# Edge preparation of a four-layer graph kernel: eight chunks staged between the given rows, tile copies two chunks behind, scratch and vectors in two parts

## The chip, the core and the metric

The program runs on one core of a Trainium2 chip. The metric is device time in microseconds (us), the median of repeated runs. The engines are PE (TensorE), PEld (its weight loads), DVE (VectorE), ACT (ScalarE), POOL (GpSimd) and SP (SyncE, which here only issues DMAs). An engine's name with a q at its end is its sequencer issuing a DMA. The lines L... are those of the kernel before.

## The reference, cut to what matters

There are 3125 nodes with 160 features, 100000 edges and four message-passing layers. Only the last steps of each layer differ in formula; all have this form:

```python
h = maximum(layernorm(x), 0)
x = x + layer(h, edge attributes, src, dst)
# in a layer: gather node rows by one index of each edge, weight them by an MLP
# of the edge attributes, multiply with the edge vector, segment_sum by the other index, mix
# layer 0: gathers by dst, sums by src, edge vector = edge_attr_3 / norm(edge_attr_3)
# layers 1 to 3: gather by src, sum by dst; dst comes sorted
```

## The kernel before

The edges stand as a grid of 128 partitions by 782 columns. Sums are made by bins of 32 nodes (100 bins), in tiles of 128 edges of one bin. A group is 8 tiles; there are 110 groups. Layer 0 needs its edge rows (69 words, `rows_a`) in order of `src`, so a preparation sorts them by counting, and scatters them to DRAM. Layers 1 to 3 need the rows (32 words, `rows_b`) in order of `dst`, in which they were given, but padded to whole tiles.

The preparation runs like this.

- DVE and PE: `count(0)` marks, for each of 100 bins, which edges fall in it (DVE, one mark a bin, a ring of 8), and PE sums the marks. Between the marks `vectors` (five steps, after marks 15, 30, 45, 60 and 75) turns the edge vectors `sh` into unit vectors, with a square root of ACT in between, and makes `key_f`. `bases(0)` makes prefix sums. `segment(i)` then ranks a range of columns: `rank` makes, for each of 100 bins, one mark on DVE, one bf16 and one f32 product on PE over the columns of the segment, and one predicated copy on DVE; `positions` turns ranks into slots. Segments are columns of chunks 0 to 3, 4 to 17 and 18 to 33 (`SEGMENTS`), a chunk being 23 columns. After segment 0 come `tiles(0)`, segment 1, `count(1)`, `bases(1)`, `tiles(1)`, segment 2, and the ranking for the other order.
- SP: `stage_rows(c)` loads the 69-word rows of chunk c into one of two buffers, once chunk c - 2 has been scattered. `given(step)` loads a chunk of 32-word rows and stores the chunk before it to `given_dram`. The two are interleaved by hand for chunks 2 to 5: ten given steps and one, then six for each chunk. Then come `bins_out(0)`, `bins_out(1)` and `starts()`, four small transfers with one word a descriptor that SP waits out, and one load back.
- From chunk 6 (`COPY_FROM`) to 33, SP and ACT each issue, for every chunk, 16 DRAM-to-DRAM copies of 128 given rows into tiles (`copy_tiles`); they read the tile starts and the given rows.
- ACT first has 30360 KB of blank rows written to the table that the scatters go to; SP's given rows and POOL's scatters wait for that write (`s_init`). `fill(c)` puts the unit vectors, the index and the key into the staged rows and writes the slots for POOL; `complete(c)` does the like for a given chunk. From chunk 18 it also prepares the node table of layer 0.
- POOL: `scatter(c)` issues 23 indirect DMAs for a chunk, in order, once its fill is done. After chunk 33 it waits for all scatters and copies, reads a flag and signals `s_placed`.
- After `s_placed` DVE clears the accumulator `acc`, all 25600 columns of it, and starts layer 0. Until then `acc` holds the preparation's scratch (`carve`). Each `acc` column is one 32-bit word of each partition.

In each layer POOL gathers rows for the 110 groups (8 indirect DMAs a group, at most two groups ahead), and PE, DVE and ACT work on them in a pipeline. SP loads the rows of group g once the gathers and selections of group g - 2 are done.

```python
acc = sb("acc", [P, BINS * 256])
    dve.wait_ge(s_placed, 1)
    ...
    link(dve.memset(acc[:, :], 0.0))
```

Of the kernel before, what the change touches and what calls it, by code (L numbers as in the profile page):

```python
# [7 lines left out]
I32 = mybir.dt.int32  # L8
# [40 lines left out]
assert BLOCKS % STORES == 0  # L49
R2, R3 = math.sqrt(2.0), math.sqrt(3.0)  # L50
assert COLS % CHUNK == 0 and CHUNKS % 2 == 0 and GROUPS % 2 == 0
SEGMENTS = (0, 4, 18, CHUNKS)
COPY_FROM = 6
GIVEN_FIRST, GIVEN_EACH = 10, 6
assert GIVEN_FIRST + GIVEN_EACH * (COPY_FROM - 2) == CHUNKS
SPREAD = TCOLS * P // (CHUNKS - COPY_FROM)
assert SPREAD * (CHUNKS - COPY_FROM) == TCOLS * P and SPREAD % (2 * GT) == 0
MARKS, PREFIXES, AHEAD = 8, 4, 4
# [1 line left out]
WORK = 2 * PRODS * 320 + 2 * 1024  # L60
assert WORK >= 2 * PRODS * 416 + 2 * 512
PREP_FROM = SEGMENTS[2]
PAD_STEP = NODES // (P * GT)


# [145 lines left out]
def gnn_program(nc, t):  # L211

    ctx = ExitStack()
    with ctx:
# [77 lines left out]
        def carve(words):  # L292
            a = used[0]
            used[0] += words
            assert used[0] <= BINS * 256
            return acc[:, a:a + words]

        even = COLS + COLS % 2
        key_i = [carve(COLS).bitcast(I32) for _ in range(2)]
        key_next = carve(COLS).bitcast(I32)  # L300
        key_f = carve(COLS)
        pos_i = [carve(COLS).bitcast(I32) for _ in range(2)]
        int_a, int_b = carve(COLS).bitcast(I32), carve(COLS).bitcast(I32)
        bin_h = [carve(even // 2).bitcast(BF16)[:, 0:COLS] for _ in range(2)]
        sh = carve(3 * COLS)
# [17 lines left out]
        tile_pad, tile_node = carve(TCOLS), carve(TCOLS)  # L323
        tile_start = carve(TCOLS).bitcast(I32)
        starts_row = carve(TCOLS * P).bitcast(I32)
        falls, unsorted = carve(1), carve(1).bitcast(I32)
        tile_id, tile_bin = carve(TCOLS), carve(TCOLS)
        tile_bin_i = [carve(TCOLS).bitcast(I32) for _ in range(2)]
        stage = [[carve(CHUNK * w) for _ in range(2)] for w in (A_W, B_W)]
        pos_r = [carve(CHUNK).bitcast(I32) for _ in range(2)]  # L330
        blank = [carve(GT * w) for w in (A_W, B_W)]


        s_src = sem("s_src")
# [132 lines left out]
        def copy_tiles(eng, kind, part, c):  # L467

            for v in range(0, SPREAD // 2, GT):
                u = part * (SPREAD // 2) + v  # L470
                _, start = nc.values_load_multi_w_load_instructions(
                    starts_row[0:1, bass.ds((c - COPY_FROM) * SPREAD + u, GT)], engines=(kind,),
                    min_val=0, max_val=P * COLS, skip_runtime_bounds_check_because="clamped to the number of edges")
                for w in range(GT):
                    eng.dma_start(tiles_b[:, bass.ds((c - COPY_FROM) * (SPREAD // GT) + u // GT, 1), w, :],
                                  given_dram[bass.ds(start[w], P), :].unsqueeze(1)).then_inc(s_copy[part], 16)
# [5 lines left out]
        def _(sp):  # L482
# [5 lines left out]
            def stage_rows(c, half, q):  # L488

                wait(sp, s_scat[q], half * (16 * CHUNK))  # L490
                sp.sem_inc(s_apart["sp"], 1)
                sp.dma_start(stage[0][q], t["rows_a"][:, bass.ds(c * (CHUNK * A_W), CHUNK * A_W)]).then_inc(s_stage[0][q], 16)
# [18 lines left out]

            sp.wait_ge(s_init, 16)
            step = 0
            for c in range(2, COPY_FROM):
                for _ in range(GIVEN_FIRST + 1 if c == 2 else GIVEN_EACH):
                    given(step, step // 2, step % 2)
                    step += 1
                stage_rows(c, c // 2, c % 2)
# [81 lines left out]

            def rows_and_tiles(c, half, q):
                stage_rows(c, half, q)
                copy_tiles(sp, SP, 0, c)
            pairs(sp, COPY_FROM, CHUNKS, rows_and_tiles)
            bins_in(0)
            edge_rows(0)
            bins_in(1)
# [166 lines left out]
        def _(act):  # L774
# [2 lines left out]
            act.dma_start(given_dram[P * COLS:, :], blank[1][:, 0:B_W]).then_inc(s_empty, 16)  # L777
            act.dma_start(rows_dram[0].rearrange("(g p t) c -> p g (t c)", p=P, t=GT),
                          blank[0].unsqueeze(1).to_broadcast([P, GROUPS, GT * A_W])).then_inc(s_init, 16)
            act.wait_ge(s_sq, 1)  # L780
            act.activation(norm, norm, ACT.Sqrt).then_inc(s_rt, 1)

            def complete(c, half, q):

# [42 lines left out]
            act.wait_ge(s_dst, 32)  # L827
            act.wait_ge(s_pos[0], 1)
            done = 0
            for c in range(COPY_FROM):  # L830
                if c == SEGMENTS[1]:
                    act.wait_ge(s_pos[0], 2)
                fill(c, c // 2, c % 2)
                if c:
                    for _ in range(GIVEN_FIRST if c == 1 else GIVEN_EACH):
                        complete(done, done // 2, done % 2)
                        done += 1
            assert done == CHUNKS

            act.wait_ge(s_empty, 16)  # L840
            for q in range(2):
# [2 lines left out]

            def fill_and_copy(c, half, q):
                fill(c, half, q)
                copy_tiles(act, ACTIVATION, 1, c)
            pairs(act, COPY_FROM, SEGMENTS[2], fill_and_copy)
            act.wait_ge(s_pos[0], 3)

            act.wait_ge(s_nodes, 32)
# [12 lines left out]
            for c in range(last, last + 2):  # L864
                fill_and_prep(c, c // 2, c % 2)
            pairs(act, last + 2, CHUNKS, fill_and_copy)

            for n in range(4):
                L, S, C = LAYERS[n], s_e[n], s_c[n]
# [115 lines left out]
        def _(dve):  # L985
            links = [0]

            def link(ins):

                links[0] += 1  # L990
                ins.then_inc(s_chain, 1)
                dve.wait_ge(s_chain, links[0])
# [42 lines left out]
                                  ALU.is_equal).then_inc(s_mark, 1)  # L1035
                marked[0] += 1

            def vectors(step):

                if step == 0:  # L1040
                    dve.wait_ge(s_vec, 16)
                    link(dve.tensor_tensor(sh2, sh, sh, ALU.mult))
                elif step == 1:
                    dve.tensor_reduce(norm, sh2.rearrange("p (e c) -> p e c", c=3), AX_X, ALU.add).then_inc(s_sq, 1)
                elif step == 2:
                    dve.wait_ge(s_rt, 1)
                    link(dve.reciprocal(norm, norm))
                elif step == 3:
                    link(dve.tensor_tensor(sh3, sh3, norm.unsqueeze(2).to_broadcast([P, COLS, 3]), ALU.mult))
                elif step == 4:  # L1050
                    link(dve.tensor_scalar(int_b, key_i[0], BIN - 1, None, ALU.bitwise_and))
                    link(dve.tensor_copy(key_f, int_b))

            def count(o):

                link(dve.tensor_scalar(int_a, key_i[o], 5, None, ALU.arith_shift_right))
                link(dve.tensor_copy(bin_h[o], int_a))
                for b in range(BINS):
                    mark(o, b, 0, COLS)
                    if o == 0 and b % 15 == 14:  # L1060
                        vectors(b // 15)

            def bases(o):

# [76 lines left out]
            def segment(i):  # L1141
# [2 lines left out]
                positions(0, a, b)  # L1144
                dve.wait_ge(s_pos[0], i + 1)
            segment(0)
            tiles(0)
            segment(1)

# [15 lines left out]
            statistics()  # L1165
            prep_first()

            for n in range(4):
                L, S, C = LAYERS[n], s_e[n], s_c[n]
                o = 0 if L.rowsA else 1  # L1170
                if n:
                    wait(dve, S["zero"], 1)
                else:

                    dve.wait_ge(s_placed, 1)
                    dve.wait_ge(s_tbd[0], 16)
                    dve.wait_ge(s_tbd[1], 16)
                    dve.wait_ge(s_startd, 32)
                    link(dve.memset(acc[:, :], 0.0))
                if n != 2:  # L1180

                    for q in range(2):
# [531 lines left out]
```

## Time and profile before

| what | value |
|---|---|
| median of 3 runs | 6038.6 us (6031.11 to 6040.99) |
| the profiled execution | 6039.14 us, of it the span 6037.4 us |
| busy share of the span | PE 75%, PEld 65%, DVE 56%, ACT 57%, POOL 70% |
| mean granted TensorE clock | 0.833 of full |
| chain that ended last | POOL 26%, issue 17%, PE 15%, DMA 13%, DVE 5% |

A busy share is an average over the preparation, the four layers and the steps between layers; what a change in one stage is worth is read in that stage. "Issue" is time in which an engine waited for nothing that the profile shows. Each engine works in program order, so a wait of one instruction holds all that stand behind it.

### The profile page before, as it was taken

The page shows a single profiled execution, that of the slowest core. Times are in us where ns is not written, and L with a number is a line of the kernel's source. Part 1 is how long each engine was busy: PE and PEld are TensorE (multiplying, and loading weights), DVE is VectorE, ACT ScalarE, POOL GpSimd, SP SyncE. Part 2 cuts the span into 40 slices and gives each one's busy share as a digit, 9 for nine tenths or more (in the row PEclk, how much of TensorE's full clock was granted, in tenths as well). Part 3 has the DMA queues.
Part 4 walks back from the last instruction along what each step waited for, and adds up shares of the span by engine and source line. Part 5 has one row for each costly group of instructions (what it writes and reads, how often), then busy time and mean ns, then how long its engine had stood idle before and what let it go on. Part 6 is the DMA issues. An engine that isn't in the chain of part 4 may idle for free.

```text
span 6037.4 us, 112434 instructions
## 1 busy us (share of the span) xinstructions
PE 4551.9 (75%) x24536; PEld 3911.6 (65%) x24536; DVE 3374.1 (56%) x10505; ACT 3437.0 (57%) x14704; POOL 4216.1 (70%) x4431
## 2 busy tenths in 40 slices
PE   8893122199999998899999985444444788888887
PEld 6552011199988887788888874444444777777776
DVE  8994000288777776566666673222222456666666
ACT  0000000066666665688888866666666577777774
POOL 4757777677777772677777747777777377777773
PEclk7996555599999999999999995555555799999998
DMA  8622333244444441233333323333333123333331
GB/s 283 192 67 72 75 83 79 56 93 93 93 93 93 93 93 26 75 78 78 78 78 78 78 54 79 78 78 78 78 78 78 40 75 78 78 78 78 78 78 45
DMA packets 660123, 507.08 MB, mean 84 GB/s; under 512 B 445302, under 2 KB 563333, under 8 KB 659894
## 3 DMA queue, kind: packets, MB, share of 16 engines
q0 software_dynamic: 195888, 316.94, 21.0%
q1 hardware_dynamic: 381782, 148.41, 10.5%
q10 hardware_dynamic: 82352, 40.52, 2.3%
q8 instruction: 46, 0.75, 0.1%
q14 instruction: 55, 0.45, 0.0%
HBM read 423.69 MB, written 96.48 MB: 86 GB/s over the span
## 4 chain that ended last, share of the span: by engine, by line
POOL 26%; issue 17%; PE 15%; DMA 13%; DVE 5%; DVEq 2%; ACT 1%; SPq 1%; POOLq 1%; ACTq 0%
POOL gath L766 26%; DMA gath<-table,rows 11%; PE bank L1582 3%; PE bank L1559 3%; DMA rows<-rows_a 2%; PE bank L1632 2%; PE bank L1584 2%; DVE work L1249 2%; PE bank L1578 2%; PE bank L1624 1%; DVE acc L1233 1%; PE bank L1535 1%; DVEq L1256 1%; DVE work L1245 1%; ACT sel L900 0%
## 5 line engine op out<-in xcount | busy, mean ns | idle before, releaser
L766 POOL DMA_INDIRECT gath<-table,rows x3520 | 3358.2, 954 | 1160.2 <-issue 1016.2
L900 ACT ACTIVATE sel<-acc,rows 128x32 f32<-128x32 f32 x10560 | 2294.4, 307 | 696.8 <-DVE acc L1224 695.5
L1233 DVE TENSOR_TENSOR acc<-acc,bank 128x160 f32 (+1 forms) x3520 | 1208.3, 343 | 1042.1 <-PE bank L1578 684.7
L1582 PE MATMUL bank<-work,sel 128*128 128x160 f32 (+1 forms) x5280 | 1335.0, 334 | 92.2 <-DVE acc L1233 91.4
L1559 PE MATMUL bank<-w,work 128*128 128x224 f32 (+2 forms) x5280 | 1160.3, 342 | 115.6 <-DVE work L1249 107.2
L1584 PE MATMUL bank<-work,sel 128*128 128x160 f32 x5280 | 1150.4, 300 | 0.0
L1559 PEld LDWEIGHTS bank<-w,work 128*128 128x128 f32 (+1 forms) x5280 | 886.3, 190 | 263.6 <-DVE work L1249 196.7
L1582 PEld LDWEIGHTS bank<-work,sel 128*128 128x128 f32 x5280 | 879.4, 190 | 191.2 <-DVE acc L1233 165.7
L697 POOL DMA_INDIRECT rows_a<-acc x782 | 760.2, 972 | 341.9 <-issue 237.2
L1578 PE MATMUL bank<-gath,sel 128*128 128x160 f32 x1760 | 549.1, 493 | 554.9 <-DMA gath<-table,rows 501.8
L1245 DVE TENSOR_TENSOR work<-bank,gath 128x256 f32<-128x256 f32 x1320 | 556.1, 421 | 719.9 <-DMA gath<-table,rows 707.6
L1584 PEld LDWEIGHTS bank<-work,sel 128*128 128x128 f32 x5280 | 909.8, 190 | 45.7
L1249 DVE TENSOR_TENSOR work<-bank,gath 128x192 f32<-128x192 f32 (+1 forms) x2640 | 896.4, 381 | 0.0
L1578 PEld LDWEIGHTS bank<-gath,sel 128*128 128x128 f32 x1760 | 462.2, 330 | 641.6 <-issue 614.2
L900 ACT ACTIVATE sel<-sel,rows 128x32 f32<-128x32 f32 x2640 | 581.9, 309 | 50.4 <-DVE sel L1224 48.1
L883 ACT ACTIVATE work<-bank 100x512 f32<-100x512 f32 (+1 forms) x440 | 250.9, 596 | 332.8 <-PE bank L1532 225.3
L818 ACT ACTIVATE acc<-acc 128x69 f32 (+1 forms) x34 | 9.3, 273 | 672.9 <-DMA acc<-in_rows_a 557.0
L1460 PE MATMUL bank<-acc,ident 100*128 100x391 f32 (+3 forms) x1000 | 374.5, 475 | 0.0
L1413 PE MATMUL bank<-ident,sel 128*64 128x128 f32 x25 | 10.2, 406 | 452.5 <-ACT sel L801 452.5
L1413 PEld LDWEIGHTS bank<-ident,sel 128*64 128x64 f32 x25 | 4.3, 174 | 455.7 <-issue 455.6
L878 ACT ACTIVATE attrT<-bank 128x256 f32<-128x256 f32 (+1 forms) x330 | 145.3, 440 | 225.4 <-PE bank L1522 206.3
L1122 DVE COPY_PREDICATED acc<-work,bank 128x391 f32<-128x391 int16 (+3 forms) x500 | 253.1, 506 | 34.0 <-PE bank L1460 29.6
(227 smaller groups left out, 3579.1 us busy)
## 6 DMA issues: line engine op xcount, KB each, us to landing
gath<-table,rows POOLq DMA_INDIRECT x3520
rows<-rows_b SPq DMA_DIRECT2D x330, 128.0 KB
rows_a<-acc ACTq DMA_DIRECT2D x1, 30360.0 KB, 101.7
rows<-rows_a SPq DMA_DIRECT2D x110, 256.0 KB
acc<-in_rows_a SPq DMA_DIRECT2D x34, 793.5 KB, 4.8
acc<-in_rows_b SPq DMA_DIRECT2D x34, 368.0 KB, 3.7
rows_given<-acc SPq DMA_DIRECT2D x34, 368.0 KB
rows_a<-acc POOLq DMA_INDIRECT x782
```

The lines of the kernel that those rows point to most:

```text
L697: pool.indirect_dma_start(rows_dram[0][:, :], bass.IndirectOffsetOnAxis(ap=pos_r[q][:, u:u + 1], axis=0), stage[0][q][:, u * A_W:(u + 1) * ...
L766: pool.indirect_dma_start(gath[q][:, u, :], None, table_dram[n][:, :], bass.IndirectOffsetOnAxis(ap=flat[:, u * w + first:u * w + first + ...
L900: i = act.activation(sel[q][:, t, at:at + BIN], hot, ACT.Copy, scale=e[:, k:k + 1])
L1122: dve.copy_predicated(pos_f[:, lo:hi], mask, bank(4 + r % PREFIXES, P, 0, hi - lo)).then_inc(s_pick, 1)
L1233: dve.tensor_tensor(sums, sums, bank(6 + b, P, 256 * h, 256 * h + L.width), ALU.add).then_inc(S["fl"].sem, 1)
L1245: dve.tensor_tensor(ps, wt[:, :, 0:128].rearrange("p h (w c) -> p h w c", w=2), two[:, :, 0:S0].unsqueeze(2).to_broadcast([P, 2, 2, S0]), ...
L1249: ins = dve.tensor_tensor(pv, wt[:, h, 128:L.wcols].rearrange("p (w m) -> p w m", w=nv) .unsqueeze(2).to_broadcast([P, nv, 3, V1]), two[:, ...
L1460: pe.matmul(out, ident[0:BINS, b:b + 1].to_broadcast([BINS, P]), base[o][0:BINS, lo:hi], start=False, stop=True).then_inc(s_prefix, 1)
L1559: ins = pe.matmul(bank(4 + u % 2, P, 224 * h, 224 * h + L.wcols), hid, w, start=True, stop=True, skip_group_check=True)
L1578: ins = pe.matmul(out, sel[qv][:, t, 0:128], gath[qv][:, t, :], start=True, stop=True, skip_group_check=True)
L1582: pe.matmul(out, sel[qv][:, t, 96:224], work[:, a + NF:a + NF + L.width], start=True, stop=False, skip_group_check=True)
L1584: ins = pe.matmul(bank(6 + b, P, 256 * h, 256 * h + NF), sel[qv][:, t, 0:128], work[:, a:a + NF], start=False, stop=True, skip_group_check ...
```

## The change

SP stages chunks 2 to 7 between the given rows, with four given steps for each chunk after the first eleven, in place of chunks 2 to 5 with six. Segment 0 becomes chunks 0 to 7 (184 columns in place of 92) and segment 1 chunks 8 to 17 (230 in place of 322). The tile copies are still 28 rounds of 32, but the round that went with chunk c now goes with chunk c + 2, and the last two follow chunk 33 on SP and on ACT. `vectors` takes a column range: columns 0 to 183 in `count(0)` as before, columns 184 to 781 in one run after segment 0; ACT takes the second square root after the fill of chunk 1, ahead of its first `complete`. The scratch is carved in another order, so that all that is in use until the last scatter lies in columns 0 to `placing` - 1 (by the widths, 2 x 23 x 69 + 2 x 23 x 32 + 2 x 23 + 8 x 69 + 8 x 32 + 782 + 1 = 6283), and DVE clears the rest once the fills and copies are done, the first 6283 after `s_placed`.

```diff
-SEGMENTS = (0, 4, 18, CHUNKS)
+SEGMENTS = (0, 8, 18, CHUNKS)
 COPY_FROM = 6
-GIVEN_FIRST, GIVEN_EACH = 10, 6
+BEHIND = 2
+GIVEN_FIRST, GIVEN_EACH = 10, 4
+VEC_CUTS = (0, SEGMENTS[1] * CHUNK, COLS)
...
+        stage = [[carve(CHUNK * w) for _ in range(2)] for w in (A_W, B_W)]
+        pos_r = [carve(CHUNK).bitcast(I32) for _ in range(2)]
+        blank = [carve(GT * w) for w in (A_W, B_W)]
+        pos_i = [None, carve(COLS).bitcast(I32)]
+        unsorted = carve(1).bitcast(I32)
+        placing = used[0]
...
-            for c in range(2, COPY_FROM):
+            for c in range(2, SEGMENTS[1]):
                 for _ in range(GIVEN_FIRST + 1 if c == 2 else GIVEN_EACH):
...
                 stage_rows(c, half, q)
+                copy_tiles(sp, SP, 0, c - BEHIND)
+            pairs(sp, SEGMENTS[1], CHUNKS, rows_and_tiles)
+            for c in range(CHUNKS - BEHIND, CHUNKS):
                 copy_tiles(sp, SP, 0, c)
-            pairs(sp, COPY_FROM, CHUNKS, rows_and_tiles)
...
+            def roots(i):
+                a, b = VEC_CUTS[i], VEC_CUTS[i + 1]
+                act.wait_ge(s_sq, i + 1)
+                act.activation(norm[:, a:b], norm[:, a:b], ACT.Sqrt).then_inc(s_rt, 1)
+            roots(0)
...
-            for c in range(COPY_FROM):
-                if c == SEGMENTS[1]:
-                    act.wait_ge(s_pos[0], 2)
+            for c in range(SEGMENTS[1]):
                 fill(c, c // 2, c % 2)
+                if c == 1:
+                    roots(1)
                 if c:
...
             assert done == CHUNKS
+            act.wait_ge(s_pos[0], 2)
...
                 fill(c, half, q)
-                copy_tiles(act, ACTIVATION, 1, c)
-            pairs(act, COPY_FROM, SEGMENTS[2], fill_and_copy)
+                copy_tiles(act, ACTIVATION, 1, c - BEHIND)
+            pairs(act, SEGMENTS[1], SEGMENTS[2], fill_and_copy)
...
             pairs(act, last + 2, CHUNKS, fill_and_copy)
+            for c in range(CHUNKS - BEHIND, CHUNKS):
+                copy_tiles(act, ACTIVATION, 1, c)
...
                     if o == 0 and b % 15 == 14:
-                        vectors(b // 15)
+                        vectors(0, b // 15)
...
             segment(0)
+            for step in range(5):
+                vectors(1, step)
             tiles(0)
             segment(1)
...
+            dve.wait_ge(s_fill[0], 4 * CHUNKS)
+            for q in range(2):
+                dve.wait_ge(s_copy[q], 16 * TCOLS * P // 2)
+                dve.wait_ge(s_tbd[q], 16)
+            dve.wait_ge(s_startd, 32)
+            link(dve.memset(acc[:, placing:], 0.0))
...
                     dve.wait_ge(s_placed, 1)
-                    dve.wait_ge(s_tbd[0], 16)
-                    dve.wait_ge(s_tbd[1], 16)
-                    dve.wait_ge(s_startd, 32)
-                    link(dve.memset(acc[:, :], 0.0))
+                    link(dve.memset(acc[:, 0:placing], 0.0))
```

## Rows read from the trace of the kernel before

**Rows 1.** Timeline of POOL: start, duration, operation, idle before it and its releaser.

```profile
127.53 1.10 POOL L697 DMA_INDIRECT rows_a<-acc  x1 [67.81 <-ACT acc L824]
...
342.38 0.97 POOL L697 DMA_INDIRECT rows_a<-acc  x1 [35.27 <-ACT acc L824]
...
1160.76 0.97 POOL L697 DMA_INDIRECT rows_a<-acc  x1 [0.30 <-issue]
```

**Rows 2.** Groups of POOL by line, 1160 to 2400: layer 0's gathers, busy, then idle.

```profile
L766 POOL DMA_INDIRECT gath<-table,rows x880 | 842.5, 957 | 289.7 <-issue 249.0 <-DMA rows<-rows_a 40.1 <-DVE work L1249 0.6
```

**Rows 3.** Timeline of DVE in count(0): three of the vector passes and the first scan.

```profile
15.67 2.60 DVE L1042 TENSOR_TENSOR acc<-acc 128x2346 f32<-128x2346 f32 x1
...
30.82 5.04 DVE L1047 RECIPROCAL acc<-acc 128x782 f32<-128x782 f32 x1
...
49.19 0.56 DVE L1051 TENSOR_SCALAR acc<-acc 128x782 int32<-128x782 int32 x1
...
60.57 1.22 DVE L1066 TENSOR_TENSOR_SCAN work<-bank,acc 100x512 f32<-100x512 f32 x1 [0.63 <-PE bank L1439]
```

**Rows 4.** Timeline of DVE in segment 0, with 92 columns.

```profile
65.33 0.86 DVE L1034 TENSOR_SCALAR work<-acc,iota_bins 128x92 bf16<-128x92 bf16 x5
...
67.08 0.26 DVE L1122 COPY_PREDICATED acc<-work,bank 128x92 f32<-128x92 int16 x1 [0.17 <-PE bank L1460]
67.25 0.24 DVE L1034 TENSOR_SCALAR work<-acc,iota_bins 128x92 bf16<-128x92 bf16 x1
```

**Rows 5.** Stretches: length, busy and count of PE, PEld, DVE, ACT, POOL; granted clock, DMA.

```profile
100.00:124.00 24.00, 24.00 (x126) 23.92 (x125) 16.26 (x79) 0.00 (x0) 0.00 (x0) 0.50 0.16 55
...
134.00:150.00 16.00, 16.00 (x71) 9.83 (x70) 15.60 (x47) 1.06 (x6) 12.24 (x13) 0.99 0.62 170
...
5000.00:5100.00 100.00, 88.85 (x537) 78.42 (x537) 63.65 (x218) 76.92 (x339) 75.78 (x80) 1.00 0.31 78
```

**Rows 6.** Timeline of PE and DVE in segment 1, with 322 columns.

```profile
130.66 0.47 PE L1459 MATMUL bank<-work,acc 128*128 128x322 bf16 x1
...
132.01 0.47 PE L1459 MATMUL bank<-work,acc 128*128 128x322 bf16 x1
...
161.00 0.52 DVE L1122 COPY_PREDICATED acc<-work,bank 128x322 f32<-128x322 int16 x1
...
161.41 0.29 DVE L1034 TENSOR_SCALAR work<-acc,iota_bins 128x322 bf16<-128x322 bf16 x1
161.62 0.52 DVE L1122 COPY_PREDICATED acc<-work,bank 128x322 f32<-128x322 int16 x1
```

**Rows 7.** Timeline of SP's DMA issues in the preparation.

```profile
104.47 0.81 SPq L499 DMA_DIRECT2D acc<-in_rows_b  x2
...
172.89 0.37 SPq L492 DMA_DIRECT2D acc<-in_rows_a  x1
...
270.02 0.37 SPq L492 DMA_DIRECT2D acc<-in_rows_a  x1
...
299.27 12.92 SPq L534 DMA_DIRECT2D tile_bins<-acc  x2
321.05 0.36 SPq L548 DMA_DIRECT2D tile_starts<-acc  x1
...
336.51 0.41 SPq L492 DMA_DIRECT2D acc<-in_rows_a  x1
...
1104.84 0.34 SPq L492 DMA_DIRECT2D acc<-in_rows_a  x1
1106.13 13.30 SPq L475 DMA_DIRECT2D rows_b<-rows_given  x16
```

**Rows 8.** Timeline of all engines at the start of layer 0.

```profile
1169.26 21.39 DVE L1179 MEMSET acc<- 128x25600 f32 x1 [127.62 <-issue]
...
1187.19 0.96 POOL L766 DMA_INDIRECT gath<-table,rows  x1 [0.30 <-issue]
...
1203.76 0.95 POOL L766 DMA_INDIRECT gath<-table,rows  x1 [15.61 <-DMA rows<-rows_a]
```

More of the change, by code:

```diff
@@ L51 @@
 assert COLS % CHUNK == 0 and CHUNKS % 2 == 0 and GROUPS % 2 == 0
-SEGMENTS = (0, 4, 18, CHUNKS)
+SEGMENTS = (0, 8, 18, CHUNKS)
 COPY_FROM = 6
-GIVEN_FIRST, GIVEN_EACH = 10, 6
-assert GIVEN_FIRST + GIVEN_EACH * (COPY_FROM - 2) == CHUNKS
+BEHIND = 2
+GIVEN_FIRST, GIVEN_EACH = 10, 4
+assert COPY_FROM + BEHIND == SEGMENTS[1] and GIVEN_FIRST + GIVEN_EACH * (SEGMENTS[1] - 2) == CHUNKS
 SPREAD = TCOLS * P // (CHUNKS - COPY_FROM)
@@ L298, in gnn_program @@
         even = COLS + COLS % 2
+        stage = [[carve(CHUNK * w) for _ in range(2)] for w in (A_W, B_W)]
[4 more added lines that the diff above has]
+        placing = used[0]
+        pos_i[0] = carve(COLS).bitcast(I32)
         key_i = [carve(COLS).bitcast(I32) for _ in range(2)]
@@ L301, in gnn_program @@
         key_f = carve(COLS)
-        pos_i = [carve(COLS).bitcast(I32) for _ in range(2)]
         int_a, int_b = carve(COLS).bitcast(I32), carve(COLS).bitcast(I32)
@@ L325, in gnn_program @@
         starts_row = carve(TCOLS * P).bitcast(I32)
-        falls, unsorted = carve(1), carve(1).bitcast(I32)
+        falls = carve(1)
         tile_id, tile_bin = carve(TCOLS), carve(TCOLS)
         tile_bin_i = [carve(TCOLS).bitcast(I32) for _ in range(2)]
-        stage = [[carve(CHUNK * w) for _ in range(2)] for w in (A_W, B_W)]
-        pos_r = [carve(CHUNK).bitcast(I32) for _ in range(2)]
-        blank = [carve(GT * w) for w in (A_W, B_W)]
         s_src = sem("s_src")
@@ L779, in _ @@
                           blank[0].unsqueeze(1).to_broadcast([P, GROUPS, GT * A_W])).then_inc(s_init, 16)
-            act.wait_ge(s_sq, 1)
-            act.activation(norm, norm, ACT.Sqrt).then_inc(s_rt, 1)
+            def roots(i):
[3 more added lines that the diff above has]
+            roots(0)
             def complete(c, half, q):
@@ L1036, in mark, with vectors @@
                 marked[0] += 1
-            def vectors(step):
+            def vectors(i, step):
+                a, b = VEC_CUTS[i], VEC_CUTS[i + 1]
+                some, squares = sh[:, 3 * a:3 * b], sh2[:, 3 * a:3 * b]
                 if step == 0:
                     dve.wait_ge(s_vec, 16)
-                    link(dve.tensor_tensor(sh2, sh, sh, ALU.mult))
+                    link(dve.tensor_tensor(squares, some, some, ALU.mult))
                 elif step == 1:
-                    dve.tensor_reduce(norm, sh2.rearrange("p (e c) -> p e c", c=3), AX_X, ALU.add).then_inc(s_sq, 1)
+                    dve.tensor_reduce(norm[:, a:b], squares.rearrange("p (e c) -> p e c", c=3), AX_X, ALU.add).then_inc(s_sq, 1)
                 elif step == 2:
-                    dve.wait_ge(s_rt, 1)
-                    link(dve.reciprocal(norm, norm))
+                    dve.wait_ge(s_rt, i + 1)
+                    link(dve.reciprocal(norm[:, a:b], norm[:, a:b]))
                 elif step == 3:
-                    link(dve.tensor_tensor(sh3, sh3, norm.unsqueeze(2).to_broadcast([P, COLS, 3]), ALU.mult))
+                    link(dve.tensor_tensor(sh3[:, a:b, :], sh3[:, a:b, :], norm[:, a:b].unsqueeze(2).to_broadcast([P, b - a, 3]),
+                                           ALU.mult))
                 elif step == 4:
-                    link(dve.tensor_scalar(int_b, key_i[0], BIN - 1, None, ALU.bitwise_and))
-                    link(dve.tensor_copy(key_f, int_b))
+                    link(dve.tensor_scalar(int_b[:, a:b], key_i[0][:, a:b], BIN - 1, None, ALU.bitwise_and))
+                    link(dve.tensor_copy(key_f[:, a:b], int_b[:, a:b]))
             def count(o):
```

## The prediction

> **What bounds the kernel now.** I read the preparation and the start of layer 0 only, since nothing behind them is edited. First POOL's timeline: 782 scatters run from 127.53 to 1161.73 with one hole, 35.27 us ahead of chunk 6 [rows 1]. Chunks 6 to 33 take (1161.73 - 342.38) / 28 = 29.26 us each; chunks 0 to 5 take (342.38 - 35.27 - 127.53) / 6 = 29.9 us each, with their small waits. So the preparation ends at: first scatter, plus 34 chunks, plus hole. DVE reaches its clearing of `acc` after idling 127.62 us [rows 8], so neither it nor the ranking for the other order sets the end; POOL does.
>
> The hole is SP's: chunk 6 is loaded at 336.51, after the given rows and the four one-word transfers, 299.27 to 336.51 [rows 7]. POOL starts 342.38 - 336.51 = 5.87 us after that load is issued.
>
> The first scatter waits for `count(0)`, `bases(0)` and segment 0 on DVE and PE, one behind the other; it can't start before the blank rows are written, about 104.47, when SP's loads start [rows 7].
>
> At the other end the clearing, 21.39 us, starts 7.5 us after the last scatter's end, and the gathers of group 2 idle 15.61 us because their rows wait for selections, which wait for the clearing [rows 8]. Later in layer 0 POOL idles little but for issue: 40.1 us on rows in all, of which 15.6 are that one wait [rows 2]. So a start that comes sooner should reach the end of the layer.
>
> **First scatter.** The vector steps in `count(0)` are three passes of 2.60, one of 5.04, two of 0.56, 13.96 us in all [rows 3] (the reduction and the scaling read as many elements as the first pass). On 184 of 782 columns that is 3.3, with some 0.15 fixed for each of six 4.0. Saved: 10.0 us. DVE stays the bound of the count: the marks between take it longer than they take PE, and only the ring's few waits are left. Ranking then starts at 65.33 - 10.0 = 55.3 [rows 4].
>
> A ranking step with 92 columns takes 24.0 / 42 = 0.57 to 0.58 us (126 products, three a step), PE and its weight loads filling the time at granted clock 0.50, the 1.2 GHz level [rows 5]; 100 steps are 58.0 us, and 127.53 - 65.33 - 58.0 = 4.2 us are head, positions, fill and issue. For 184 columns no row exists. At the low level a step of 322 columns takes 132.01 - 130.66 = 1.35 us [rows 6], and by columns 184 take 0.77. At the high level DVE is the longer one: its copy takes 0.17 us at 92 [rows 4] and 0.41 at 322 [rows 6], so 0.27 at 184; its mark takes (0.86 - 0.24) / 4 = 0.155 at 92 and 0.21 at 322, so 0.18; together 0.45. PE would want 0.38. So segment 0 is 77 us at the low level and 45 at the high. Which? The 92-column steps never left the low level; the 322-column steps began at it and were at 0.99 from 134 on [rows 5], a few us after the first of them. In time by columns 184 at the low level is 0.77 us of streaming without room for more, as at 322, and unlike 92, where the loads filled the step. I take the high level after six steps at the low one: 6 x 0.77 + 94 x 0.45 = 46.9, and 4.7 for the rest (positions are twice as wide). First scatter: 55.3 + 46.9 + 4.7 = 106.9, just past the floor of 104.47. Gain 20.6 us; the bounds are +22 and, at the low level throughout, -9.5 (137.0).
>
> The second part of the vectors, 598 columns, some 11 us, runs after segment 0. Behind it on DVE are `tiles(0)` and segment 1, which chunk 8 needs 240 us later: covered. ACT's second root stands ahead of the first `complete`, behind two passes of 2.0 us, so the given rows start some 4 us later against the first scatter. They were ten steps and 172.89 - 127.53 = 45.4 us to chunk 2's load; now 49.1, plus 5.9 to the scatter, is 55.0 where chunk 2 is due at 59.8. Covered, thinly. That DVE's passes slow the scatters beside them costs 0 to 4 us; I take 0, as the pace of 29.9 has DVE's work in it.
>
> **The hole.** Between the loads of chunks 2 and 5 three cycles of six given steps take (270.02 - 172.89) / 3 = 32.4 us [rows 7], so four take 21.6, less than a chunk's scatter: each load now waits for its buffer instead. Chunk 7 is loaded when chunk 5 is scattered, at 106.9 + 6 x 29.9 + 1.6 = 287.9 (1.6 is from the scatter's end to the load, as at 1104.84 = 1161.73 - 2 x 29.26 + 1.6). Four given steps follow, two thirds of 299.27 - 270.02, 19.5: 307.4. Then the one-word transfers: 37.2 us before, but the first of them, with scatters beside it, took 12.5 us where the second took 8.9 (321.05 - 299.27 - 12.92, with its issue 9.2) [rows 7]. Now all have scatters beside them. Bounds: 37 and 50; I take 41.8. Chunk 8 is loaded at 349.2 and scattered from 355.1. It is due at 106.9 + 8 x 29.9 = 346.1. Hole: 9.0 us in place of 35.3. From there 26 x 29.26 = 760.8: end 1115.9, 45.8 us sooner than 1161.73.
>
> Tile copies do not open the hole again: 1.3 + 13.3 us a round [rows 7] in 29.26. The last two rounds stand behind chunk 33's load, 56.9 us before POOL ends: SP is through three rounds after 43.8 us, ACT, whose fill comes first, after some 48.4, and landed by some 51. POOL's wait for copies is covered by about 6 us.
>
> **The clearing.** 21.39 us for 25600 columns is 0.836 ns each: 16.1 us for the first 19317, 5.3 for the last 6283. The first part starts some 6 us before POOL ends (P) and ends at P + 10.1, past `s_placed` at P + 7.5; the second ends at P + 15.6 where the clearing ended at P + 28.9. Gain 13.3 us, of at most 16.1; group 2's gathers keep 2.3 us of their 15.61.
>
> The Trainium skill, "VectorE: DVE Perf Modes", section "Zero memsets can be issued as uint32 (trn2)", says that a memset takes one cycle per element; that would be an estimated 20.1 and 6.5 us at its 0.96 GHz, and a gain of some 8 in place of 13.3. The row of 21.39 us decides against it.
>
> **Sum.** 45.8 + 13.3 = 59.1 us from the profiled execution's 6039.1, which stands within 0.5 us of the median 6038.6: 5980.
>
> **The rivals.**
> - The clock stays low in segment 0: first scatter at 137.0, all else as above: 5980 + 30 = 6010. For it: the 92-column steps, low from end to end. Against: 322. Chance 0.15.
> - The change moves the hole rather than closing it: given steps or one-word transfers stretch beside the scatters (six given steps took 32.4 us in the mean of three cycles and 29.3 in the last, so the pace is not fixed). At 50 us for the transfers 5988; if the whole 35.3 us came back, 6006. Chance 0.12.
> - DVE's first clearing stops POOL's scatters: up to 16 us, 5996. Against: a gather during the clearing took 0.96 us, its usual 957 ns [rows 8, 2]. Chance 0.03. By the Trainium skill, "SBUF — State Buffer", section "Who interferes with whom", a DVE instruction with at most one SBUF input does not contend outside its two-port modes; the trace agrees.
> - Slower than before: a layer that now comes 59 us sooner loses the high clock. Layer 3 has PE at 88.85 us of 100 at clock 1.00 [rows 5]; at the low level the same work is 177.7, so each 100 us cost 78 more, and from 76 us at the low level the gain is gone: 200 us would give 6136. Against: those loops aren't edited. Chance 0.03.
>
> My forecast has 0.67. The range holds the forecast's own bounds (22 in place of 20.6 for the first scatter, a hole of 4, all 16.1 of the clearing: 5971, with a few us of spread), and reaches over the first rivals: 5967 to 6012. A measurement of this kernel tells 0.2%, 12 us, from no change; beyond that on the fast side lie nearly all cases: faster 0.94, same 0.02, slower 0.04.
>
> **What would show it.** POOL's first scatter near 107 (137: the clock); DVE's copies of 184 columns every 0.45 us from about 61; SP's load of chunk 8 near 349 and the idle ahead of POOL's next scatter under 15 us; scatters ending near 1116; two memsets of 16 and 5 us, the second ending 16 us after the last scatter; every layer as long as before. A hole over 20 us, or a first scatter past 115, makes the sum wrong.

## The result and the profile after

| | before | changed | predicted |
|---|---|---|---|
| median | 6036.13 us (4 runs beside it) | 5985.23 us (4 runs, 5982.02 to 5992.07) | 5980 |
| ratio | 1 | 0.9917 [0.99, 0.9934] | 0.990 |
| profiled execution, span | 6039.14, 6037.4 us | 5982.02, 5980.4 us | |
| mean granted TensorE clock | 0.833 | 0.838 | |
| first scatter | 127.53 | 107.07 | 106.9 |
| hole: idle ahead of the first scatter behind the one-word transfers | 35.27 | 7.66 | 9.0 |
| last scatter ends (P) | 1161.73 | 1114.48 | 1115.9 |
| clearing ends behind P | 28.9 | 21.4 | 15.6 |

The kernel is faster by 0.8%: 50.9 us by the medians, where the sum said 59.1. The profiled executions differ by 57.1 us, because the one before stood 3.0 us above its median and the changed one 3.2 below its own. Positions below are those of the profiled executions. The table's lower four rows tell where the sum held and where it did not: three of them are within 1.5 us, the last is off by 5.8.

POOL's timeline in the changed kernel, the rows that answer to [rows 1] and [rows 8]:

```profile
107.07 1.23 POOL L704 DMA_INDIRECT rows_a<-acc  x1 [44.54 <-ACT acc L834]
...
353.65 0.97 POOL L704 DMA_INDIRECT rows_a<-acc  x1 [7.66 <-ACT acc L834]
...
1113.52 0.97 POOL L704 DMA_INDIRECT rows_a<-acc  x1 [0.30 <-issue]
...
1149.23 0.95 POOL L773 DMA_INDIRECT gath<-table,rows  x1 [8.59 <-DMA rows<-rows_a]
```

The first row came 20.5 us sooner, the hole shrank by 27.6, and P came 47.25 us sooner, 0.8 us less than their sum. The idle ahead of group 2's gathers, 15.61 us before, is 8.59 where 2.3 was forecast.

DVE's timeline from the end of the count to the second part of the vectors:

```profile
39.36 8.45 DVE L1047 TENSOR_SCALAR work<-acc,iota_bins 128x782 bf16<-128x782 bf16 x25
48.47 1.23 DVE L1082 TENSOR_TENSOR_SCAN work<-bank,acc 100x512 f32<-100x512 f32 x1 [0.66 <-PE bank L1461]
...
53.12 0.97 DVE L1047 TENSOR_SCALAR work<-acc,iota_bins 128x184 bf16<-128x184 bf16 x5
...
57.87 0.37 DVE L1138 COPY_PREDICATED acc<-work,bank 128x184 f32<-128x184 int16 x1 [0.29 <-PE bank L1482]
58.13 0.26 DVE L1047 TENSOR_SCALAR work<-acc,iota_bins 128x184 bf16<-128x184 bf16 x1
58.58 0.37 DVE L1138 COPY_PREDICATED acc<-work,bank 128x184 f32<-128x184 int16 x1 [0.18 <-PE bank L1482]
...
60.98 0.37 DVE L1138 COPY_PREDICATED acc<-work,bank 128x184 f32<-128x184 int16 x1
61.24 0.26 DVE L1047 TENSOR_SCALAR work<-acc,iota_bins 128x184 bf16<-128x184 bf16 x1
61.45 0.37 DVE L1138 COPY_PREDICATED acc<-work,bank 128x184 f32<-128x184 int16 x1
...
103.37 0.26 DVE L1145 CAST acc<-acc 128x184 int32<-128x184 f32 x1
...
105.30 2.03 DVE L1057 TENSOR_TENSOR acc<-acc 128x1794 f32<-128x1794 f32 x1
...
117.26 0.26 DVE L1103 COPY acc<-bank 128x100 f32<-128x100 f32 x1
```

The first scan starts 12.1 us sooner than in [rows 3] (10.0 in the sum), and the 100 steps of segment 0 take from 53.12 to 103.37, 50.2 us (46.9 in the sum). The second part of the vectors takes 105.30 to 117.26, behind segment 0, as said.

DVE's groups by line in the changed kernel, 50 to 104 (busy, mean ns of one, then idle):

```profile
L1138 DVE COPY_PREDICATED acc<-work,bank 128x184 f32<-128x184 int16 x100 | 36.5, 365 | 2.5 <-PE bank L1482 2.1
L1047 DVE TENSOR_SCALAR work<-acc,iota_bins 128x184 bf16<-128x184 bf16 x100 | 26.3, 266 | 0.0
```

Stretches of the same kernel (PE, PEld, DVE, ACT, POOL, granted clock, DMA):

```profile
55.00:60.00 5.00, 5.00 (x26) 4.13 (x24) 3.65 (x15) 0.00 (x0) 4.34 (x9) 0.67 1.09 372
60.00:65.00 5.00, 5.00 (x37) 4.26 (x36) 5.00 (x22) 0.00 (x0) 2.12 (x6) 1.00 1.06 385
65.00:103.00 38.00, 37.59 (x243) 26.69 (x241) 37.29 (x159) 0.00 (x0) 0.00 (x0) 1.00 1.02 365
```

Here the choice between the two levels of the clock can be read: it rises inside the first stretch, with PE busy throughout, and stays at 1.00, the 2.4 GHz level, to the end of the segment. The rows before show the same from DVE: in the first steps its copy waits for PE, 2.1 us in all; from about 59 on it waits for nothing and starts a copy every 0.47 us.

SP's issues around the old hole, answering to [rows 7]:

```profile
306.21 13.80 SPq L539 DMA_DIRECT2D tile_bins<-acc  x2
330.86 0.36 SPq L553 DMA_DIRECT2D tile_starts<-acc  x1
331.27 0.56 SPq L554 DMA_DIRECT2D tile_first_node<-acc  x1
345.52 0.29 SPq L556 DMA_DIRECT2D acc<-tile_starts  x1
347.99 0.40 SPq L497 DMA_DIRECT2D acc<-in_rows_a  x1
```

From 306.21 to 347.99 are 41.8 us, the value taken (the load back of the starts is in it); chunk 8 is loaded 1.2 us sooner than forecast.

The chain that ended last, at the clearing, in the changed kernel (start, length, what):

```profile
1106.33 2.34 DMA rows_b<-rows_given
...
1108.92 4.10 issue
1113.02 16.17 DVE acc L1191
1129.19 1.36 issue
1130.55 5.30 DVE acc L1201
```

and the same chain in the kernel before:

```profile
1163.87 5.39 issue
1169.26 21.40 DVE acc L1179
```

The last tile copy had landed at 1108.7, 5.8 us ahead of P; the forecast had 6. But each memset has "issue" ahead of it, 4.10 and 1.36 us, together the 5.5 us that the sum lacks. What that is became the main question.

Layer 0 handed the gain on. The first row of the memset that follows it on POOL, before and after:

```profile
2310.70 2.77 POOL L738 MEMSET acc<- 128x3200 f32 x1 [16.68 <-PE bank L1624]
```

```profile
2255.13 2.77 POOL L745 MEMSET acc<- 128x3200 f32 x1 [16.68 <-PE bank L1646]
```

It starts 55.6 us sooner, where 47.25 + 7.5 = 54.75 came in at the layer's start. No layer lost the high clock that it had before.

### The profile page after: what moved, and what is told of

Its sections match the earlier page's. It is cut to its first block, busy times and chain, and to the rows that moved or that the text cites. A ratio compares the mean times of both kernels' runs of the same rounds, so it can differ in the third digit from the quotient of the medians.

```text
span 5980.4 us, 112354 instructions
## 1 busy us (share of the span) xinstructions
PE 4519.9 (76%) x24536; PEld 3884.8 (65%) x24536; DVE 3365.0 (56%) x10512; ACT 3432.8 (57%) x14705; POOL 4219.0 (71%) x4431
## 4 chain that ended last, share of the span: by engine, by line
POOL 37%; issue 21%; DMA 16%; PE 14%; DVE 7%; DVEq 2%; SPq 1%; ACT 1%; ACTq 1%; POOLq 1%
POOL gath L773 26%; DMA gath<-table,rows 12%; POOL rows_a L704 11%; DMA rows<-rows_a 3%; PE bank L1654 2%; PE bank L1604 2%; DVE work L1271 2%; PE bank L1581 2%; PE bank L1600 2%; PE bank L1606 2%; PE bank L1646 1%; DVE acc L1255 1%; DVE work L1267 1%; DVEq L1278 1%; PE bank L1557 1%
## 5 line engine op out<-in xcount | busy, mean ns | idle before, releaser
L1482 PE MATMUL bank<-acc,ident 100*128 100x391 f32 (+3 forms) x1000 | 349.5, 441 | 0.0
```

Of the source, the lines that this page charges most:

```text
L1482: pe.matmul(out, ident[0:BINS, b:b + 1].to_broadcast([BINS, P]), base[o][0:BINS, lo:hi], start=False, stop=True).then_inc(s_prefix, 1)
```

## The experiments

The kernels come in three sets of four; the first two sets ran on one chip, the third on another. Each set's ratios are against the kernel before in the same set (6038.93, 6036.76 and 6036.36 us). POOL's gathers of layer 0 take 967 to 974 ns on the first chip and 955 to 959 on the second, so positions are compared within a chip. Which chip the result above comes from is not on record. Its gathers (957 ns before, 956 after) and its transfers (41.8 us; 37.7 to 38.7 in five kernels on the first chip, 41.2 and 42.3 in two on the second) are like the second's, and it is compared with that one.

**One part undone at a time** (first set). Segment 0 back to chunks 0 to 3, with eight chunks staged all the same:

```diff
-SEGMENTS = (0, 8, 18, CHUNKS)
+SEGMENTS = (0, 4, 18, CHUNKS)
+STAGED = 8
...
+                if c == SEGMENTS[1]:
+                    act.wait_ge(s_pos[0], 2)
                 fill(c, c // 2, c % 2)
```

> The changed kernel, but segment 0 has 92 columns again (segment 1 has 322); SP still stages chunks 2 to 7, the vectors stay in two parts. Theory (clock): ranking 92 columns stays at the low clock and takes 58 us where 184 columns took 50, so the first scatter comes near 115 in place of 107.07, and all behind it, the scatters' end included, some 8 us later; total about 8 us above the changed kernel. Rival (work): half the columns are half the work, ranking takes about 33 us and the first scatter waits only for the blank rows, near 107; total unchanged.

Measured 5998.76 us, 0.9934 [0.992, 0.9947]. POOL's first scatter, and the stretch of the ranking, in this kernel:

```profile
115.48 1.24 POOL L705 DMA_INDIRECT rows_a<-acc  x1 [51.50 <-ACT acc L835]
```

```profile
65.00:103.00 38.00, 38.00 (x199) 37.81 (x198) 26.90 (x132) 0.00 (x0) 0.00 (x0) 0.50 1.02 366
```

Half the columns take longer: the 92-column steps stay at granted clock 0.50, the 1.2 GHz level, with PE and its loads full, and last 0.58 us where the 184-column steps last 0.47. The hole was only 3.87 us here, so P was 1118.97. The repeat of the changed kernel on this chip (below) has 108.34, 4.85 and 1113.97: 7.1 us at the first scatter became 5.0 at P, the rest was given back by the shorter hole and the pace of the scatters.

The vectors in one part:

```diff
-VEC_CUTS = (0, SEGMENTS[1] * CHUNK, COLS)
+VEC_CUTS = (0, COLS)
...
-            for step in range(5):
-                vectors(1, step)
```

> The changed kernel, but the vectors are made in one part, all columns inside count(0). Theory: the count is bound by DVE, so the first scatter comes 10 us later, near 117, the second root no longer stands ahead of the given rows, the hole ahead of chunk 8 stays 7 to 8 us, total 10 us above the changed kernel. Rival: PE or the blank rows bound the count as well and the first scatter moves by under 4 us.

Measured 6001.35 us, 0.9934 [0.992, 0.9948]; first scatter 119.13, hole 5.10 (7 to 8 was expected, but the repeat has 4.85 too), P 1124.24. Against the same repeat the split is worth 10.8 us at the first scatter and 10.3 at P.

The scratch cleared in one part:

```diff
-            link(dve.memset(acc[:, placing:], 0.0))
...
-                    link(dve.memset(acc[:, 0:placing], 0.0))
+                    link(dve.memset(acc[:, :], 0.0))
```

> The changed kernel, but acc is cleared in one piece after the last scatter. Theory: the clearing ends 28.9 us after the last scatter's end as before, in place of 21.4, the gathers of group 2 idle 15.6 us in place of 8.6, total 7.5 us above the changed kernel. Rival: the start of layer 0 is bound by its gathers and the split is worth nothing, total within 2 us.

Measured 5999.67 us, 0.9932 [0.9919, 0.9946]. P was 1114.17; DVE's timeline:

```profile
1121.69 21.39 DVE L1197 MEMSET acc<- 128x25600 f32 x1 [125.95 <-issue]
```

It starts at P + 7.5 and ends at P + 28.9, as before the change. Against the repeat (P + 21.7) the split is worth 7.2 us at this place, against the profiled changed kernel 7.5, and not the 13.3 of the sum.

The first part cleared without waiting for the tile copies, which takes the row of starts that they read (896 words) into the last part, 7179 columns:

```diff
+        starts_row = carve(TCOLS * P).bitcast(I32)
         placing = used[0]
...
-                dve.wait_ge(s_copy[q], 16 * TCOLS * P // 2)
```

> The changed kernel, but the tile starts that the copies read lie in the part cleared last (7179 columns), so the first clearing (18421 columns) waits for the fills and not for the copies. Theory: it starts 52 us before the last scatter ends and is hidden whole, the second (6.0 us) starts 7.5 us after that end and ends 13.5 us after it, total 7.9 us below the changed kernel. Rival (port): a clearing of 15.4 us beside scatters stops POOL for as long, the chunk it falls in takes 45 us in place of 29.3, total 7 us above the changed kernel.

Measured 5987.79 us, 0.9913 [0.99, 0.9927]. The memsets in this kernel:

```profile
1063.68 15.41 DVE L1190 MEMSET acc<- 128x18421 f32 x1 [70.27 <-issue]
1115.59 6.04 DVE L1200 MEMSET acc<- 128x7179 f32 x1 [36.51 <-issue]
```

The large one now lies 48 us ahead of P (1111.83), beside running scatters. These kept their pace, 13 of them from 1063 to 1079 at 966 ns with 0.30 between: DVE's clearing does not stop POOL's scatters. The clearing ends at P + 9.8, where 13.5 was expected: that took the 7.5 us between P and the memset as fixed, and they became 3.8. The time fell less than expected all the same, as the repeat shows.

**Repeat, and one part alone** (second set).

> The changed kernel once more, on the chip of the three below, so that they are compared with it and not across chips. First scatter near 107, last scatter's end near 1114, clearing done 21.4 us after it; about 0.992 of the time of the kernel before. The four runs of the first call gave 0.9934, 0.9934, 0.9932 and 0.9913; if clear_without_copies is 8 us below this kernel, this one stands near 0.9926, and if the first clearing stood in the way of the scatters there, near or below 0.9913.

Measured 5992.14 us, 0.9922 [0.9909, 0.9936]. First scatter 108.34, hole 4.85, P 1113.97; the clearing again ends 21.7 us behind P, with 1.38 us between its parts. On this chip the four kernels above are thus 6.6, 9.2 and 7.5 us slower and 4.4 us faster than the changed kernel by their medians. They belong to another set, whose kernel before was 2.2 us slower, and by the ratios the intervals overlap, so these differences are good to a few us; the positions in the traces carry the readings. The repeat gained 44.6 us on its kernel before and not 50.9.

> The kernel before with nothing but the other order of the scratch and the clearing in two parts. There the copies are through 42 us before the last scatter ends. Theory: the first clearing (16.2 us) is over before it, the second (5.3 us) ends about 13 us after it in place of 28.9, group 2's gathers wait little; total 14 to 16 us below the kernel before (0.9975). Rival (late copies are no cause): here too the clearing ends 21 us after the last scatter, total 7 us below.

This is the kernel before with the scratch carved in the new order and cleared in two parts. Measured 6024.58 us, 0.9978 [0.9969, 0.9987]. The copies are long done here, so the first part (1121.46) is hidden and the clearing ends at P + 8.9 in place of P + 28.9. P itself was 1153.28 and the hole 27.29 us, though nothing ahead of the clearing was edited but the places in the scratch: SP's transfers began at 293.48, 5.8 us sooner than in [rows 7], and took 33.7 us in place of 37.2. This is the other chip, and no trace of the kernel before was taken there, so whether the chip or the scratch's order makes the 8 us stays open. The total fell by 12.2 us, near the 14 to 16 expected.

**The one-word transfers issued together.** Each order's wait for its bins is moved behind the issue of all four:

```diff
                     sp.dma_start(bins_dram[o].rearrange("(c p) -> p c", p=P), tile_bin_i[o]).then_inc(s_tbd[o], 16)
-                sp.wait_ge(s_tbd[o], 16)
...
             starts()
+            for o in range(2):
+                sp.wait_ge(s_tbd[o], 16)
```

> The changed kernel, but SP issues the four one-word transfers one behind the other and waits once, in place of waiting out each pair. Theory (the hole is the sum of three waits): the transfers take 15 to 25 us in place of 42, chunk 8 is loaded by 331 and waits for nothing, POOL's hole of 7.7 us is gone, all behind it 7 us sooner. Rival (descriptors): the four share the same queue and take their 38 us all the same, hole and total unchanged.

Measured 5986.32 us, 0.9915 [0.9902, 0.9929]. SP's timeline:

```profile
307.37 1.14 SPq L539 DMA_DIRECT2D tile_bins<-acc  x2
308.56 0.71 SPq L552 DMA_DIRECT2D tile_starts<-acc  x1
309.31 0.58 SPq L553 DMA_DIRECT2D tile_first_node<-acc  x1
328.38 0.30 SPq L555 DMA_DIRECT2D acc<-tile_starts  x1
332.82 0.40 SPq L497 DMA_DIRECT2D acc<-in_rows_a  x1
```

With three waits between them (one behind each order's bins, one behind the last two) the four transfers and the load back took 37.7 us in the repeat; beside one another they take 25.5, and the hole is gone: no wait over 0.4 us stands ahead of chunk 8, and P is 1108.70, 5.3 us sooner than in the repeat.

> The changed kernel with both: transfers together, and the first clearing free of the copies. Theory: the two add, the scatters end 7 us sooner and group 2's gathers follow group 1's without a wait, total 15 us below the changed kernel. Rival: one hides the other (gathers of layer 0 bound it from its start), total 8 us below.

These are the transfers together and the first part cleared without the copies. Measured 5982.07 us, 0.9909 [0.9894, 0.9924], 10.1 us under the repeat of the changed kernel, between the theory's 15 and the rival's 8. P came 5.4 us sooner and the clearing's end another 11.9 nearer to it. Layer 0, from P to the memset behind it, took 1151.4 us in the repeat and 1146.45 here: of the 11.9 us 4.9 reached its end. Both mechanisms worked at their own place, but the layer does not hand on the whole of the second.

**Staging alone, and what the clearing waits for** (third set, the other chip).

> The changed kernel with the vectors in one part, the scratch cleared in one part and the old bounds of the segments (0, 4, 18, 40): SyncE's staging and the trailing copies are all that is left of the change. If the three parts add up, the first scatter starts near 127 us and the stop between scatters, 27 to 28 us long before, shrinks to under 6; POOL's scatters then end 20 to 25 us sooner than before's, near 1137 to 1142, the clearing starts 7.5 us behind them as before, and the time is 20 to 30 us below before's, ratio .995 to .997. A rival: the stop stays above 15 us although eight chunks are staged, because the first scatters come as late as before; then the ratio is above .997.

Measured 6008.28 us, 0.9956 [0.9943, 0.997], a little better than expected, though the hole is longer than the 6 forecast: first scatter 127.35, hole 7.75, P 1133.63, 28.1 us sooner, and the medians differ by 28.1 too. Of the 54.75 us at the start of layer 0 staging with the trailing copies thus brings 28.1, and what is left, 1133.63 - 1114.48 = 19.2 at P and 7.5 in the clearing, belongs to the other parts. That this adds up is no test, since the 19.2 is a difference. Undone one at a time on the first chip, the segment and the vectors gave 5.0 and 10.3 at P, and 7.1 and 10.8 at the first scatter, of 20.3 here. The trailing of the copies was never undone by itself.

The next kernel asks whether the 4.1 us ahead of the first memset are the price of DVE's 116 us without work:

```diff
                 copy_tiles(sp, SP, 0, c)
+            sp.sem_inc(s_wake, 1)
             bins_in(0)
...
+            dve.wait_ge(s_wake, 1)
+            link(dve.memset(acc[:, placing:placing + 1], 0.0))
             for q in range(2):
                 dve.wait_ge(s_copy[q], 16 * TCOLS * P // 2)
```

> The changed kernel with one signal from SyncE behind its last tile copy, on which VectorE clears one word before it waits for the rest. Theory: the 4.1 us between the last landing and the first memset is the price of a long sleep, whatever the instruction is; the one word's memset pays it, beginning some 4 us after the signal, near 1108.7, and the first part's memset follows at once, within 1 us of the last copy's landing, 3 to 4 us sooner than in the changed kernel; the clearing ends near 17.5 to 18.5 us behind the last scatter in place of 21.4, and the time falls by 2 to 4 us. Rival: the 4 us is between the copies' landing and what a wait sees of it; then the one word is cleared within 0.5 us of the signal and the first part's memset stays 4 us behind the landing.

Measured 5984.71 us, 0.9918 [0.9904, 0.9931], no change. SP's and DVE's timelines:

```profile
1105.25 0.40 SPq L548 DMA_DIRECT2D tile_bins_row<-tile_bins  x1
```

```profile
1105.32 0.06 DVE L1190 MEMSET acc<- 128x1 f32 x1 [108.12 <-issue]
1112.78 16.16 DVE L1195 MEMSET acc<- 128x19317 f32 x1 [7.40 <-issue]
1130.32 5.29 DVE L1205 MEMSET acc<- 128x6283 f32 x1 [1.38 <-issue]
```

The theory falls. SP signals between its last copy's issue (over at 1105.14) and the issue at 1105.25, and after 108 us without work the one-word memset starts 0.07 us behind the latter. The large one still starts 4.3 us behind the last landing (1108.44); DVE's waits take the first 0.2 of them, and the other 4.10 are "issue", as before. The rival named beside it fits this kernel, but not the one after the next.

> The kernel with both mends, and the same signal from SyncE, some 4 us before the last scatter: VectorE clears one word on it and then waits for POOL. Theory of the long sleep: the one word's memset starts some 4 us behind the signal, the second part's memset within 0.5 us of POOL's mark in place of 3.75 behind it, the clearing ends 6.5 us behind the last scatter in place of 9.8, and the time falls by another 1 to 3 us, since the gathers' pace already sets the layer's start. Rival, the delay belongs to the wait for POOL's mark: the second memset stays 3.7 us behind.

Measured 5973.27 us, 0.9893 [0.9877, 0.9908], no gain over the kernel without it. SP's signal came just ahead of 1098.81 here, 10 us ahead of P and not 4, and the one word was cleared at 1098.88; the second part still started 3.8 us behind P.

> The kernel with both mends once more, for a comparison on the same chip: as before, a ratio of .991 and a second memset that starts 3.75 us behind the last scatter's end.

Measured 5971.29 us, 0.9891 [0.9876, 0.9906], the best of all, 13.4 us under the changed kernel with the one-word memset, measured beside it. The second memset starts 3.77 us behind P, as expected. ACT's last fill and DVE's memsets in this kernel:

```profile
1057.17 0.20 ACT L835 ACTIVATE acc<-acc 128x23 int32<-128x23 int32 x1
```

```profile
1061.28 15.41 DVE L1191 MEMSET acc<- 128x18421 f32 x1 [70.09 <-issue]
1112.98 6.04 DVE L1201 MEMSET acc<- 128x7179 f32 x1 [36.29 <-issue]
1119.24 0.70 DVE L1205 MEMSET sel<- 128x768 f32 x1 [0.23 <-DVE acc L1201]
```

Here the signal is ACT's and no DMA's, and the large memset still starts 1061.28 - 1057.37 = 3.91 us behind the end of ACT's last fill. So the wait for a landing is not it either. What orders all rows is the size of the memset itself:

```
columns   ahead of the row (us)   row (us)   together   what came just before
25600     5.39                    21.39      26.78      POOL's signal
19317     4.10                    16.16      20.26      last copy landed
18421     3.91                    15.41      19.32      ACT's last fill
 6283     1.36                     5.29       6.65      the first part's memset
  768     0.23                     0.70       0.93      a memset
    1     0.07                     0.06       0.13      SP's signal
```

The share ahead of the row is 0.21 to 0.22 ns a column in the four large ones, whoever released them and after 116 us of idle or none. It goes with the memset's size, and the row shows only four fifths of what the memset costs: 26.78 / 25600 = 1.046 ns a column here. The memset of 7179 columns, not in the table, fits: POOL's signal came 2.14 us behind P in the kernel before (1163.87 in the chain above), 7179 x 0.21 ns are 1.5, together 3.6, and it starts 3.75 and 3.77 us behind P.

## Why the prediction held, and where it did not

**First scatter: right, by errors that cancel.** The count gained 12.1 us, not 10.0. The vector passes themselves came out as worked out (0.72, 0.72, 1.30, 0.73, 0.25 and 0.26, 3.98 in all). The other 2.1 us are DVE's few waits in the ring of marks, which the sum kept and which are gone: every 15 marks now take 5.09 us, and the last 25 take 8.45 where they took 9.56. Segment 0 took 50.2 us, not 46.9: the low steps lasted 0.83 us (0.77 in the sum) and the high ones 0.47 (0.45), a mark 0.21 where the sum had put 0.18 between the ends of [rows 4] and [rows 6]; the copy's 0.26 is the sum's 0.27. What follows the ranking took 3.7 us, not 4.7. So 2.2 us too late, 3.3 too short and 1.0 too long make the 0.2 by which the first scatter was missed: that closeness is luck. The choice that carried the step, the high level after about six steps, was right, and the undone segment shows what it was worth.

**The hole: right.** Chunk 7's load at 288.10 (287.9), the transfers from 306.21 (307.4) and their 41.8 us are the sum's. The repeat had a hole of 4.85 us with the same code and transfers of 37.7, so the size is known to some 3 us only, and that 41.8 was met to the tenth is luck. That they take longer in the new order was right on both chips, 37.2 to 41.8 here and 33.7 (the scratch's order alone) to 37.7 on the first. The mechanism, transfers waited for one behind the other, is shown by issuing them together: 37.7 to 25.5 us on the first chip, 41.2 and 42.3 to 29.1 and 31.7 (the two kernels with both mends) on the second.

**The copies: right.** They landed 5.8 us ahead of P where 6 was worked out, and POOL never waited for them.

**The clearing: the step that failed.** "21.39 us for 25600 columns is 0.836 ns each" took the row's length for the memset's cost. The mechanism was right: the first part starts when the copies land and the second follows it. The size was not: the two parts cost 20.26 + 6.65 us and not 16.1 + 5.3. With them the first part ends at 1108.7 + 20.3 = P + 14.5 (measured 14.7) and the second at P + 21.1 (measured 21.4), and the gain over 28.9 is 7.5 us. In the kernel before, 5.39 us of the 7.5 between P and the memset of [rows 8] are this same share, and the sum gave all 7.5 to `s_placed`; by the chain above POOL's signal comes at P + 2.14. The two errors are one. It also made the gathers of group 2 wait 8.59 us and not 2.3.

The Trainium skill, "VectorE: DVE Perf Modes", section "Zero memsets can be issued as uint32 (trn2)", has a memset at one cycle per element; the prediction set it aside because of the row's 21.39 us. The measurements agree with the page: its estimated 20.1 and 6.5 us for the two parts stand against 20.26 and 6.65, and the gain of some 8 us that it gave against 7.5.

**The layer behind it: right in this kernel.** Of 54.75 us at the start of layer 0, 55.6 arrived at its end. That is one pair of executions: the kernel before and staging alone clear alike, at P + 28.9, and their layers take 1149.0 and 1147.1 us. It does not hold for every lead. On the second chip the clearing ended 28.9, 20.7 and 9.8 us behind P in three kernels (staging alone, the changed kernel with the one word, both mends again), and layer 0 took 1147.1, 1141.1 and 1133.0 us from P: 8.2 us gave 6.1, the next 10.9 gave 8.1. On the first chip it is sharper: with the clearing in one part (P + 28.9) the layer took 1159.5 us, with it in two (P + 21.7) 1151.2 to 1151.4 in four kernels, and with the first part hidden (P + 9.8 and P + 8.9) 1146.5 to 1147.2 in three. So the first 7.2 us came through whole, and of the next 11.9 4.9. POOL's groups in layer 0, 1120 to 2230, for the kernel with both mends, on the first chip and then on the second:

```profile
L774 POOL DMA_INDIRECT gath<-table,rows x870 | 846.0, 972 | 265.1 <-issue 255.7 <-DMA rows<-rows_a 9.5
```

```profile
L774 POOL DMA_INDIRECT gath<-table,rows x877 | 838.5, 956 | 267.3 <-issue 245.3 <-DMA rows<-rows_a 21.6 <-DVE work L1271 0.3
```

With the clearing out of the way, POOL's own gathers are what is left: 846 of 1110 us busy and nearly all the rest "issue", the 0.30 us between one gather and the next. A lead then only helps as far as the gathers can use it. Whether an earlier start itself slows the gathers (968 ns in the repeat, 972 here) is not settled: on the second chip they take 955 to 959 with no such order.

**The rivals.** The clock rose, so 6010 fell. The hole did not come back. The clearing beside the scatters cost them nothing. No layer lost the high level. What the sum had wrong was none of them but a size inside the likeliest case: 5.8 us lost in the clearing. Between the profiled executions 1.4 of them came back at P, nearly all by the hole (7.66 in place of 9.0), and some 2.4 in layer 0 and behind it, about as much as layer 0 varies; so 57.1 stands near 59.1 in part by luck. By the medians the gain is 50.9, 8.2 us short: the 5.8 of the clearing account for most of it. On the first chip it is 44.6. The repeat's layer 0 took 1151.4 us where the changed kernel above took 1140.7, with the slower gathers; yet the kernel before is as fast on both chips (6036.76 and 6036.36 us). With no trace of it from the first chip, why the change is worth less there stays open.

## What to carry to other kernels

An "issue" ahead of a long instruction after a wait is not always slack: see whether it grows with the instruction's size, in several kernels or rows, before it is counted as fixed or as somebody else's delay. Small transfers on one queue that do not need one another's results are issued first and waited for together (12 us of 38 here). And ask of every wait in front of a clearing which of the buffers it really guards: here 896 words held back 18421 columns.

## What the runs showed of the hardware

- A DVE memset of f32 zeros costs 1.046 ns a column, of which its row in the profile shows 0.836 (21.39 us for 25600 columns); the remaining 0.21 stands as idle "issue" ahead of it. Where the instruction really begins inside that time no run shows.
- DVE needs next to no time to come back from a long wait: after 108 us its one-word memset began within 0.2 us of the signal.
- A ranking step on 92 columns takes 0.58 us and on 184 columns 0.47, because the first stays at the 1.2 GHz level and the second rises to 2.4 GHz after six steps.
- Four one-word transfers and a load back cost 25.5 us issued together and 37.7 with three waits between them, on the same chip.
- The same kernel's indirect gathers (both mends) took 972 ns on one chip and 956 on another; the ends of its layer 0 stand 12.9 us apart (2255.06 and 2242.18), as much as the two mends bring (10.1 and 13.4 us). Kernels are compared on one chip.
